# Adding the FFN's down columns by accumulating transfers, and moving the third column's scaling from VectorE to ScalarE

## What is computed

```
def _L1_ffn_ref(x, gate_w, gate_z, gate_s, up_w, up_z, up_s, down_w, down_z, down_s):
    def dequantize(imatrix, scales, zeros, group_size, out_dtype):
        ...   # (imatrix - zeros) * scales, one zero and one scale for each group of 128 rows
    gate = silu(x @ gate_proj)        # 512 -> 1792
    up = x @ up_proj                  # 512 -> 1792
    return (gate * up) @ down_proj    # 1792 -> 512
...
x = x + _L1_ffn_ref(_layernorm(x), ...)
```

## Time and profile before

| | |
|---|---|
| time, median of 3 runs | 837.85 us (837.78 to 839.21) |
| the profiled execution's own time | 838.27 us |
| its span, first to last instruction | 836.5 us |
| mean granted TensorE clock | 0.996 |
| busy share of the span: PE, DVE, ACT, POOL | 98%, 68%, 64%, 66% |
| busy in 90 us of the FFN (700 to 790 us): PE, DVE, ACT, POOL | 89.97, 88.58, 64.78, 86.80 us |

### The profile page before, as it was taken

One profiled execution on the slowest core, in us unless ns is written; L12 is line 12 of the kernel. 1 busy time (PEld: TensorE's weight loads), 2 busy tenths in 40 slices (PEclk: granted clock), 3 DMA queues, 4 the chain that ended last, 5 costly groups with the idle time before them and its releaser, 6 DMA issues.

```text
span 836.5 us, 13343 instructions
## 1 busy us (share of the span) xinstructions
PE 819.1 (98%) x3952; PEld 676.3 (81%) x3952; DVE 565.4 (68%) x993; ACT 536.3 (64%) x1773; POOL 551.3 (66%) x555
## 2 busy tenths in 40 slices
PE   9999999999899999999999999999999999999995
PEld 7887888888788888888888888888887777777774
DVE  6516755433566666666666666666568899999996
ACT  4633652245677777777777777777677467677763
POOL 3432642322587777777777777777676268999996
PEclk9999999999999999999999999999999999999999
DMA  9412667105666666666667766666754023444302
GB/s 321 152 39 59 158 170 195 50 1 154 181 183 192 185 188 187 188 187 186 187 190 227 226 190 188 187 185 196 231 158 142 1 82 145 152 151 152 133 19 101
DMA packets 96199, 130.02 MB, mean 155 GB/s; under 512 B 25792, under 2 KB 68672, under 8 KB 96128
## 3 DMA queue, kind: packets, MB, share of 16 engines
q1 hardware_dynamic: 96128, 129.18, 51.5%
HBM read 90.08 MB, written 39.06 MB: 154 GB/s over the span
## 4 chain that ended last, share of the span: by engine, by line
PE 91%; DVE 3%; POOL 2%; ACT 2%; DMA 1%; issue 1%; SPq 0%; POOLq 0%; ACTq 0%; DVEq 0%
PE pair L1667 21%; PE pair L1669 21%; PE pair L1668 21%; PE pair L1835 9%; PE pair L1836 8%; PE pair L1929 6%; PE pair L1689 1%; PE pair L1731 1%; PE pair L1782 1%; PE pair L1759 1%; DVE kv L1267 1%; DMA land<-block_bounce 0%; DMA kv<-in_ctxT_dram 0%; DVE kv L1588 0%; DVE resid L1467 0%
## 5 line engine op out<-in xcount | busy, mean ns | idle before, releaser
L1667 PE MATMUL pair<-split,xnT_hi 128*128 128x512 f32 x288 | 112.5, 391 | 0.3 <-issue 0.3
L1669 PE MATMUL pair<-split,xnT_lo 128*128 128x512 f32 x288 | 112.1, 389 | 0.0
L1668 PE MATMUL pair<-split,xnT_hi 128*128 128x512 f32 x288 | 112.1, 389 | 0.0
L1005 ACT ACTIVATE headT<-land,wqk 128x512 f32<-128x512 f32 x62 | 44.9, 724 | 93.5 <-DMA land<-block_bounce 76.7
L1667 PE MATMUL pair<-split,aoT_hi 128*128 128x512 f32 x244 | 96.4, 395 | 0.5 <-DVE resid L1467 0.5
L1669 PE MATMUL pair<-split,aoT_lo 128*128 128x512 f32 x244 | 95.7, 392 | 0.0
L1668 PE MATMUL pair<-split,aoT_hi 128*128 128x512 f32 x244 | 95.4, 391 | 0.0
L1026 ACT ACTIVATE prob<-pair,nmax 128x128 f32<-128x128 f32 x244 | 85.9, 362 | 12.3 <-DVE nmax L1445 12.1
L1835 PE MATMUL pair<-xnT_hi,split 128*128 128x512 f32 x224 | 90.7, 405 | 2.0 <-DVE kv L1588 1.2
L774 POOL TENSOR_TENSOR prob<-prob,rinv 128x512 f32<-128x512 f32 x61 | 63.6, 1043 | 39.7 <-DVE rinv L1415 39.7
L1836 PE MATMUL pair<-xnT_lo,split 128*128 128x512 f32 x224 | 87.6, 391 | 0.0
(11 more groups left out here) (202 smaller groups left out, 2165.8 us busy)
## 6 DMA issues: line engine op xcount, KB each, us to landing
block_bounce<-tb SPq DMA_DIRECT2D x244, 128.0 KB, 2.3
land<-block_bounce SPq DMA_DIRECT2D x61, 512.0 KB, 3.4
raw<-in_wqo_dram SPq DMA_DIRECT2D x62, 256.0 KB, 3.0
kv<-in_ffn_w_dram SPq DMA_DIRECT2D x14, 768.0 KB, 4.4
kv<-in_ffn_z_dram SPq DMA_DIRECT2D x14, 768.0 KB, 5.7
kv<-key_bounce SPq DMA_DIRECT2D x32, 128.0 KB, 2.9
key_bounce<-tb SPq DMA_DIRECT2D x44, 64.0 KB, 2.1
resid<-in_x_dram SPq DMA_DIRECT2D x2, 1024.0 KB, 8.2
```

The lines of the kernel that those rows point to most:

```text
L1667: pe.matmul(dst, l_hi, r_hi, start=first, stop=False)
L1668: pe.matmul(dst, l_hi, r_lo, start=False, stop=False)
L1669: return pe.matmul(dst, l_lo, r_hi, start=False, stop=last)
```

## The change

ScalarE takes E2 as well, right behind G0, scaled into `tmp_c` (which only the end of the FFN used so far). VectorE doesn't take it any more. GpSimd's additions to `accT` in the units become transfers that add to their destination, three a unit instead of two: 128 x 1024 fp32, 512 KB, from the scratch tile to `accT[:, c, :]`. The semaphore of a transfer counts 16 when it has landed, so all waits on those semaphores are in steps of 16 (`LANDED`). In unit i GpSimd's order becomes `sub_down`, `hidden_lo`, `sub_gate`, issue column 2, issue column 3, `sub_up`, issue column 0. ScalarE waits before E2 until the last transfer from `tmp_c` has landed, and before E3 and D0 as before, now for landings. The last additions after the units stay tensor_tensor instructions, with semaphores of their own.

```
-        V_POS, A_POS = (1, 2, 4, 5, 7, 8, SIDE), (0, 3, 6, 9)
+        V_POS, A_POS = (2, 4, 5, 7, 8, SIDE), (0, 1, 3, 6, 9)
...
             def add_down(i, p, c):
                 n = unit_at(p, i)
-                if c == 0:
-                    pool.wait_ge(s_ta, by_scalar(n + 1, 9))
-                else:
-                    pool.wait_ge(s_ta, by_scalar(n + 2, 3))
-                tmp, done = (tmp_a, s_pa) if c == 0 else (tmp_b, s_pb)
-                pool.tensor_tensor(accT[:, c, :], accT[:, c, :], tmp, ALU.add).then_inc(done, 1)
+                pool.wait_ge(s_ta, by_scalar(n + 1, 9) if c == 0 else by_scalar(n + 2, 1 if c == 2 else 3))
+                tmp, done = {0: (tmp_a, s_pa), 2: (tmp_c, s_p2), 3: (tmp_b, s_pb)}[c]
+                pool.dma_start(accT[:, c, :], tmp, accum_op=ALU.add).then_inc(done, LANDED)
...
                 if p is not None or i >= 3:
+                    add_down(i - 2, p, 2)
                     add_down(i - 2, p, 3)
...
             def last_added(e, h, c):
-                tmp, done = (tmp_a, s_pa) if c == 0 else (tmp_c, s_pb)
+                tmp, done = (tmp_a, s_la) if c == 0 else (tmp_c, s_lc)
                 pool.wait_ge(s_ta, by_scalar(LAST, 9) + 3 + e)
-                pool.wait_ge(done, LAST - 1)
+                if c == 0:
+                    pool.wait_ge(s_pa, LANDED * (LAST - 1))
+                else:
+                    pool.wait_ge(s_p3, 1)
...
                 take(i, p, 0, gated(par), gu_s[:, par, 0:1])
+                if not skipped(i, p, 1):
+                    if i == 2:
+                        act.wait_ge(s_ds, 1)
+                    elif p is not None or i >= 4:
+                        act.wait_ge(s_p2, LANDED * (n - 3))
+                    take(i, p, 1, accT[:, 2, :] if p is None and i == 2 else tmp_c, down_s[:, par, 2:3])
                 hidden_hi(i - 1, p)
...
-                        act.wait_ge(s_pb, n - 3)
+                        act.wait_ge(s_pb, LANDED * (n - 3))
...
-                    act.wait_ge(s_tv, by_vector(n, 1))
+                    act.wait_ge(s_tv, by_vector(n - 1, SIDE))
...
-                    act.wait_ge(s_pa, n - 2)
+                    act.wait_ge(s_pa, LANDED * (n - 2))
...
             take(LAST, None, 9, tmp_a, down_s[:, 1 - LAST % 2, 0:1])
+            act.wait_ge(s_p2, LANDED * (LAST - 2))
             take(LAST, None, SUM, tmp_c, down_s[:, 1 - LAST % 2, 1:2])
...
                 dve.wait_ge(s_gs, n + 1)
-                if not skipped(i, p, 1):
-                    take_down(i, p, 1, 2, p is None and i == 2)
```

More of the change, by code:

```diff
@@ L411, in cross_attention_ffn @@
         s_pb = sem("down_added_from_b")
+        s_p2 = sem("down_added_from_c")
+        s_p3 = sem("last_down_three_added")
+        s_la = sem("last_half_added_from_a")
+        s_lc = sem("last_half_added_from_c")
         s_p1 = sem("last_down_one_added")
@@ L476, in cross_attention_ffn @@
         OUT_POOL = (1, 3, 5)
+        LANDED = 16
         def skipped(i, p, pos):
@@ L485, in item @@
             return 6 * KT + 2 + ITEMS * (n - 2) + pos + 1
-        V_POS, A_POS = (1, 2, 4, 5, 7, 8, SIDE), (0, 3, 6, 9)
+        V_POS, A_POS = (2, 4, 5, 7, 8, SIDE), (0, 1, 3, 6, 9)
         def by_vector(n, pos):
             if isinstance(n, int) and n == 1:
-                return 6 + sum(k != 1 for k in V_POS if k <= pos)
+                return 6 + sum(k <= pos for k in V_POS)
             return 12 + len(V_POS) * (n - 2) + V_POS.index(pos) + 1
@@ L497, in by_scalar @@
             if isinstance(n, int) and n == 1:
-                return 8 + sum(k != 3 for k in A_POS if k <= pos)
+                return 8 + sum(k not in (1, 3) for k in A_POS if k <= pos)
             return 11 + len(A_POS) * (n - 2) + A_POS.index(pos) + 1
@@ L855, in _ @@
             pool.wait_ge(s_ta, by_scalar(LAST, 9) + 2)
-            pool.tensor_tensor(accT[:, 3, :], accT[:, 3, :], tmp_b, ALU.add).then_inc(s_pb, 1)
+            pool.wait_ge(s_pb, LANDED * (LAST - 2))
+            pool.tensor_tensor(accT[:, 3, :], accT[:, 3, :], tmp_b, ALU.add).then_inc(s_p3, 1)
             for e, (h, c) in enumerate(((0, 0), (0, 3))):
@@ L1225, in _ @@
             last_hi(1)
-            act.wait_ge(s_pb, LAST - 2)
+            act.wait_ge(s_pb, LANDED * (LAST - 2))
             act.wait_ge(s_it, item(LAST, 13))
@@ L1232, in _ @@
                 if e == 0:
-                    act.wait_ge(s_pa, LAST - 1)
+                    act.wait_ge(s_pa, LANDED * (LAST - 1))
                 else:
@@ L1640, in _ @@
             dve.wait_ge(s_it, item(LAST, 12))
+            dve.wait_ge(s_p2, LANDED * (LAST - 2))
             dve.scalar_tensor_tensor(out=accT[:, 2, :], in0=pair[pair_of(LAST, None, 12)][:], scalar=down_s[:, 1 - LAST % 2, 2:3],
@@ L1647, in _ @@
                 if c == 0:
-                    dve.wait_ge(s_pa, LAST - 1)
+                    dve.wait_ge(s_pa, LANDED * (LAST - 1))
                 if c == 1:
@@ L1651, in _ @@
                 if c == 3:
-                    dve.wait_ge(s_pb, LAST - 1)
+                    dve.wait_ge(s_p3, 1)
                 dst = accT[:, c, half(h)]
@@ L2080, in _ @@
                     pe.wait_ge(s_tv, by_vector(LAST, 8) + 1 + (2, 6)[h])
-                    pe.wait_ge(s_pa, LAST)
-                    pe.wait_ge(s_pb, LAST)
+                    pe.wait_ge(s_la, 1)
+                    pe.wait_ge(s_lc, 1)
                 for c in range(KT):
```

## The result

The changed kernel takes 867.89 us (median of 4 runs, 866.6 to 869.9) against 837.82 us of the kernel before (4 runs): a ratio of 1.0354, 95% interval 1.034 to 1.0368. That is slower, as forecast, and by 30 us where 9 were forecast; 867.9 lies above the range, which ended at 860.

What follows compares the result with a forecast made beforehand. TensorE was bound at 11.31 us a unit by stalls behind VectorE; the new E2 wait makes a 12.45 us loop. Nine periods +10.3, two others -0.8, end -0.6: +8.9, 846.8 us; range 840 to 854, all cases 832 to 860.

Steps and rivals of the forecast that it cites:

- E2: The taking of column 2 in each unit, moved from VectorE (1.19 us freed) to ScalarE (1.10 us added), behind G0.
- The floor and the gain: TensorE's 48 matmuls take 10.90 us a unit against 11.31 now; E2 off VectorE is worth at most 0.41 us a unit.
- GpSimd's issue: Issuing one transfer from GpSimd was taken as 1.0 us, giving GpSimd 9.1 us a unit, under TensorE's 10.90.
- Rival B: GpSimd's issues are dear, 2.4 us each, so GpSimd needs 13.3 us a unit: about 862 us; chance 0.10.
- The loop's fixed part: From ScalarE's E2 through hidden_hi, hidden_lo and sub_gate to the issue of column 2's transfer: 5.75 us.
- Two reads: An adding transfer reads source and destination, so its 512 KB take 2.4 us of DMA time, not 1.2.
- What is beside it: Loads with 2.4 us still to come share the DMA engines with column 2's addition, stretching it to 4.2 to 4.8 us.
- L: Time from issue to landing of column 2's transfer: forecast 6.4 to 7.0, taken as 6.7 us; full gain needs 5.15.
- even sharing: Loads and addition split the DMA engines equally, both taking twice their time: 4.8 us for the addition.
- The end: GpSimd's last column 0 addition, on the chain that ended last, becomes an issue: -0.6 us, between 0 and -0.7.
- Rival A: Column 2's transfer lands in time, L below 5.15 us, TensorE's 10.90 us a unit holds: 832.7 us; chance 0.32.

Runs made afterwards that it cites:

- two tiles and GpSimd's column 0: Changed kernel with a second scratch tile each for columns 2 and 3 by turns, column 0 added by GpSimd's tensor_tensor: 834.12 us, ratio 0.9958 to the kernel before.
- plain copies: Changed kernel with the three transfers of a unit as plain copies in place of additions: 855.78 us, ratio 1.0208 to the kernel before.
- short loads: Changed kernel with weight and zero loads of units 2 to 13 cut to 128 of 1536 columns: 836.33 us, ratio 0.9975 to the kernel before.
- early-issue kernel: Changed kernel with column 2's transfer issued ahead of hidden_lo in GpSimd's order, not behind hidden_lo and sub_gate: 844.51 us, ratio 1.0079 to the kernel before.

## Why the prediction was right in kind and wrong in size

*The floor and the gain.* 10.90 us a unit from seventeen matmuls held: 10.88 in unit 3 of the changed kernel, 10.88 again with two tiles and GpSimd's column 0. E2 off VectorE is worth what was said, once nothing else is in the way.

*GpSimd's issue.* Taken as 1.0 us. In the changed kernel the issues of columns 2 and 3, 0.6 us apart, are followed by a subtraction of 1.9 in place of 1.3 us. From 745.88 to the end of that subtraction at 748.95 are 3.07 us, 1.3 of it the subtraction's, so 0.9 each. Rival B is out.

*The loop's fixed part.* 5.75 forecast, 5.81 measured. Which wait, behind which instruction, in which units, came out as written, and so did what happens where no loads fly: the transfer issued in unit 12 landed in 4.6 us, as forecast.

*Two reads.* 2.4 us were taken for an addition, 2.66 measured, 2.06 times the copy. The Trainium skill's rule (Collectives: The Full Stack, "The bandwidth ceiling") that two sources halve the rate is what the traces show here too, for an addition within SBUF. The Trainium skill's fit of 2.0 us and the bytes at 436 GB/s (DMA: Bandwidth & Descriptors, "Anatomy of one DMA — SWDGE (gpsimd) path"), an estimate of 3.2 us, is below all that the adding transfers took, the shortest of any kernel here being 4.5 us. For a copy the trace agrees better: the first plain copy issued with nothing else in flight, at 821.51 us of that kernel, landed in 2.9 us.

*The step that failed is "What is beside it".* I let the transfer share the engines with the loads, evenly or 4 to 3, without loss: 2.4 us of load and 2.4 us of addition, so 4.2 to 4.8 us for its bytes, and L = 6.7. The DMA view of the changed kernel shows something else. Column 2's transfer was issued at 760.25, the loads (q1) at 758.84 and 759.37. From 762 to 765 us:
```profile
q1 hardware_dynamic: 159, 0.85, 100.8%
q0 software_dynamic: 5, 0.02, 3.4%
```
From 765 to 768 us:
```profile
q0 software_dynamic: 152, 0.58, 96.9%
q1 hardware_dynamic: 20, 0.06, 4.8%
```
Five of the addition's packets start while 159 of the loads' do, and most of it moves when they are done. The last packet of the loads ends at 765.74, 5.5 us after the issue; 2.66 us of the addition's own bytes make 8.2, and it landed after 8.3. Over the nine units it landed 1.9 to 3.1 us behind the second load, 2.5 us in the median. The plain copies (shorter by their own bytes alone) and the short loads (at most 4.9) both fit this, and even sharing fits neither the packets nor the copies.

But waiting behind the loads isn't by itself what I missed. With loads of 2.4 us still to come it gives 2.4 + 2.4 us and the landing, 7.0 us, which is the same as even sharing, the top of my 6.4 to 7.0. What had no term is that the loads got slower while they held the addition up: their second transfer landed 7.1 us after its issue (median of nine), where the kernel before has 5.7. Of the 2.0 us between 6.7 and the measured 8.7 this is about 1.4; the addition's own bytes, 2.66 in place of 2.4, are 0.3, and 0.3 is that I took 6.7 and not 7.0. At L = 8.7 the prediction's own loop gives 5.8 + 8.7 = 14.5 us for the 14.45 measured, and nine periods 2.0 longer are 18 us of the 21 that were missing.

*The rest.* The end gained nothing where 0.6 was forecast: from the taking of G0 of unit 13 to the last instruction it is 29.3 us, before it 29.1. The prediction had the transfer from tmp_c of unit 13 land 0.1 us before ScalarE wants the tile. It landed 5.1 us after its issue at 841.25, and ScalarE stood still for 1.57 us at 846.37, then for 0.36 and 1.45 us behind the landings for its next two takings. About 1 us lies ahead of unit 2 (G0 at 684.04, before at 683.01), where both kernels have the same code; I have no cause for it. And the median of the changed kernel's runs lies 1.3 us above its profiled execution.

*The chances.* Rival A (0.32) rested on the same unseen thing as the forecast, what loads and an addition do to each other, and no row of the trace before held two queues at once. For the same reason nothing in the ranges, up to L = 7.5 for the forecast alone, allowed for loads that get slower. The direction and the place of the loss were reasoned and came out; the size of L was a guess at something that no row showed.

## What to carry to other kernels

Work handed from a busy engine to a transfer comes back as latency: before the share of engine time, look for the instruction that waits for the landing and follow who stands behind it; if the transfer's own issue does, the flight is part of the period. A second scratch tile by turns takes the flight out of the loop (868 to 841 us here, same transfers), and then the engines' throughput decides how many such transfers fit (three a unit no, two yes: 834 us). For the flight's upper bound, put it behind everything else that is in flight, and don't take those transfers at their undisturbed pace: here that sum gave 7.0 us, and 8.3 to 9.2 were measured.

## What the runs showed of the hardware that was not expected

- Transfers that add, from GpSimd's queue, hardly moved while SyncE's loads were in flight, though issued only 1.4 us after the first of these. Why isn't shown: the loads slowed down at the same time (289 GB/s from 762 to 765 us against the plateau of 437; one packet of 6 KB took 0.23 us in the kernel before, and 0.38 to 0.48 us in the mean from 763 to 764.5 us here), so something did share the engines with them, of which the packets tell nothing. It isn't the addition's second read: beside plain copies the second load also landed in 7.1 us (median). And it isn't a fixed order of the queues: in the early-issue kernel, where additions were under way when the loads came, packets of both went through side by side, and the second load landed in 10.0 us.
- Loads and additions together moved 264 GB/s in two kernels with the engines full; 3.6 + 3 x 2.66 = 11.6 us of work a unit would be 271.
- TensorE's clock fell. Up to 741 us it was busy for 3.61 of 6 us and then waited 2.74 us for ScalarE's E2; the two stretches behind it (columns as in the earlier trace rows):
```profile
741.00:748.00 7.00, 6.65 (x17) 5.16 (x18) 2.34 (x2) 6.06 (x10) 5.68 (x5) 0.53 0.75 200
748.00:754.00 6.00, 6.00 (x28) 4.95 (x27) 5.35 (x6) 2.24 (x2) 3.15 (x3) 1.00 0.91 230
```
  Matmuls started every 0.43 us in the first, up to 747.5 us, and every 0.22 to 0.24 in the second, at 1.2 and 2.4 GHz. The unit, at 14.3 us from E2 to E2, was no longer than the others: TensorE was done with its E2 at 752.7, and ScalarE waited for the transfer until 754.50 all the same.
